# A transformer-like network with two mixtures of experts: a region of memory for each expert, routing and sending in groups of 8 tiles, expert tiles of 128 rows whose results are scattered inside the loop, plain loads in the combine

## The reference, cut to what matters

```python
def _moe(tokens, router_w, w1, b1, w2, b2):            # layer 0: hidden width 256
    logits = tokens @ router_w.T
    probs = softmax(logits); rw, re = top_k(probs, 2)
    rw = rw / maximum(rw.sum(-1), 1e-12)
    out = tokens
    for e in range(8):
        h = gelu(tokens @ w1[e] + b1[e]); y = h @ w2[e] + b2[e]
        out = out + combine[:, e:e+1] * y               # combine: rw at the two experts, else 0
# layer 1: hidden width 1024, logits = x @ Wg + bg, shares = softmax of the two best logits,
#          out = sum of share * (gelu(x @ W1[e] + b1[e]) @ W2[e] + b2[e])
x = x + attention0(ln_c(x));  t = tokens(x);  t = t + moe0(ln_t(t))
x = x + attention1(ln_c(x));  t = tokens(x);  t = t + moe1(ln_t(t));  return image(t)
```

## Time and profile before

| | us |
|---|---|
| median of 3 runs | 2737.84 |
| the profiled execution | 2757.99 |
| its span (first to last instruction) | 2756.3 |
| TensorE busy | 2073.8 (75%) |
| VectorE busy | 2053.9 (75%) |
| ScalarE busy | 1503.3 (55%) |
| GpSimd busy | 908.0 (33%) |
| mean granted TensorE clock | 0.859 of full speed |

### The profile page before, as it was taken

The page is one execution under the profiler, slowest core; times in us unless marked ns, Lnnn a source line. Parts: engine busy times, 40 slices in busy tenths (PEclk is TensorE's granted clock), DMA queues, the critical chain, the costliest instruction groups (busy, mean ns, idle before and its releaser), DMA issues. The chain is left out here.

```text
span 2756.3 us, 80547 instructions
## 1 busy us (share of the span) xinstructions
PE 2073.8 (75%) x26686; PEld 1558.4 (57%) x26687; DVE 2053.9 (75%) x3051; ACT 1503.3 (55%) x1982; POOL 908.0 (33%) x1023
## 2 busy tenths in 40 slices
PE   4639999999999999999770593036983079999961
PEld 3327666666666666666550472013862069999951
DVE  4979999999999999999782365487985334454433
ACT  5339999999999999999421120022532233333311
POOL 2652111121111111111036445460124844455455
PEclk8869999999999999999855797557975589999975
DMA  1001111111111111111204353200003611111123
GB/s 73 0 23 31 30 30 30 30 29 27 29 29 29 30 30 30 30 30 33 66 1 162 118 159 113 75 1 1 0 0 133 232 60 46 47 52 46 46 77 126
DMA packets 235071, 147.07 MB, mean 53 GB/s; under 512 B 151873, under 2 KB 214417, under 8 KB 234769
## 3 DMA queue, kind: packets, MB, share of 16 engines
q1 hardware_dynamic: 201520, 92.48, 12.9%
q0 software_dynamic: 12288, 33.57, 3.7%
q10 hardware_dynamic: 21216, 20.45, 2.1%
HBM read 70.52 MB, written 51.64 MB: 44 GB/s over the span
## 5 line engine op out<-in xcount | busy, mean ns | idle before, releaser
L579 DVE TENSOR_TENSOR plow<-prob 128x1024 f16<-128x1024 f32 (+1 forms) x1024 | 1128.0, 1174 | 4.9 <-ACT prob L493 4.9
L493 ACT ACTIVATE prob<-scores 128x1024 f32<-128x1024 f32 x1024 | 999.1, 1026 | 91.0 <-PE scores L622 63.3
L642 PEld LDWEIGHTS outp<-vs,prob 128*128 128x128 bf16 x7680 | 516.2, 98 | 277.7 <-issue 215.7
L642 PE MATMUL outp<-vs,prob 128*128 (+1 forms) x7680 | 604.4, 193 | 26.8 <-DVE plow L579 15.9
L622 PE MATMUL scores<-qT,kT 128*128 (+1 forms) x2048 | 611.6, 380 | 7.6 <-DMA kT<-shift_rows 2.8
L644 PE MATMUL outp<-vs,plow 128*128 (+1 forms) x7680 | 601.8, 193 | 0.0
L644 PEld LDWEIGHTS outp<-vs,plow 128*128 128x128 f16 x7680 | 503.4, 97 | 59.4 <-issue 0.5
L441 POOL TENSOR_TENSOR osum<-osb 128x128 f32<-128x128 f32 x64 | 105.2, 1643 | 957.3 <-DVE rec L584 957.3
L1338 ACT ACTIVATE m1ehf<-m1eph,m1eb1c 128x256 f32<-128x256 f32 x312 | 144.8, 475 | 269.5 <-PE m1eph L1294 269.2
L1400 POOL TENSOR_TENSOR m1ehl<-m1ehf,m1ehh 128x256 f16<-128x256 f32 x312 | 211.6, 709 | 219.3 <-DVE m1ehh L1369 219.3
L1294 PE MATMUL m1eph<-m1exT,m1w 128*128 128x256 f16 x1872 | 212.3, 274 | 0.2 <-DVE m1exT L1363 0.2
(11 more groups left out here) (343 smaller groups left out, 3290.3 us busy)
## 6 DMA issues: line engine op xcount, KB each, us to landing
m1estg<-in_L_ffn_W_dram SPq DMA_DIRECT2D x16, 1024.0 KB
sorted_rows<-zero SPq DMA_DIRECT2D x64, 156.0 KB
m0exr<-sorted_rows SPq DMA_DIRECT2D x39, 256.0 KB, 2.7
expert_rows<-m0eyo ACTq DMA_DIRECT2D x39, 256.0 KB, 2.3
m1exr<-sorted_rows SPq DMA_DIRECT2D x39, 256.0 KB, 3.3
expert_rows<-m1eyo ACTq DMA_DIRECT2D x39, 256.0 KB, 3.8
staged<-qk SPq DMA_DIRECT2D x73, 128.0 KB, 2.5
tok<-in_x_dram SPq DMA_DIRECT2D x4, 1024.0 KB, 10.2
```

The costliest lines, as they stand in the source:

```text
L493: act.activation(prob[g % PBUF][:, :], scores[g % 2][:, :], ACT.Exp, scale=1.0 / (QK_SCALE * QK_SCALE)).then_inc(prob_ready, 1)
L579: dve.tensor_tensor(l[:, 0:n], p[:, 0:n], high(p)[:, 0:n], ALU.subtract).then_inc(low_ready, 1)
L642: pe.matmul(to, high(prob[g % PBUF])[:, cols], v, start=(g == 0 and i == 0 and j == 0), stop=False, skip_group_check=True)
```

## The change

Both MoE are rebuilt, with the same arithmetic on the rows:

- **Regions.** `sorted_rows` is no longer one packed list: each expert has a region of 4096 rows, one such tensor for each MoE (2 x 32896 rows). A row's place is its expert's region plus its rank there, which needs only the tokens before it. A row is 1044 bytes: the two halves, the code of the expert as first choice, and 4 copies of a target number (twice the token's number, plus one place's offset of spare rows for each of 4 buffers). Zeros now fill 2 x 534 KB for each chunk in the attention, issued at the same place.
- **`dispatch`** takes the place of norm, logits, routing, sending and weight loading, in one block. Per tile ScalarE normalizes and copies, VectorE makes both halves, TensorE transposes in float16 and multiplies by the gate. After each 8 tiles (with a lead of 3 tiles) VectorE runs the routing chain for these 8, on 128 x 64, TensorE ranks them, and GpSimd scatters them; rows lie in a ring of 16. Between the groups come weight parts (16 of 256 KB in the first MoE, two after each of the first three groups; 32 of 512 KB in the second, five after each), the rest after the last group.
- **The loop** runs over 71 tiles of 128 rows, with four buffers. SP reads a tile's first row from a table into a register. VectorE has the low halves too, and ScalarE the copy of the transposed rows. VectorE computes the 128 target rows (`aim`), and GpSimd scatters the results to `expert_rows` at 2 x token + choice (L1487). `aim` waits until the scatter that used the same buffers, four tiles ago, has landed. The load of the second bias stands at the start of this block.
- **The combine** loads plainly, 8 DMAs of 1 MB by SP in three buffers.

The diff, cut to its core:

```diff
-            def zero_rows(c):
-                sp.dma_start(sorted_dram[ds(c * ZP * ZROWS, ZP * ZROWS), :].rearrange("(p a) c -> p a c", a=ZROWS),
-                             zero[0:ZP, :, :]).then_inc(zeroed, 16)
+                for rows in sorted_rows:
+                    sp.dma_start(rows[ds(c * P * ZROWS, P * ZROWS), :].rearrange("(a p) c -> p a c", p=P),
+                                 zero[:, :, :].broadcast_to([P, ZROWS, RW])).then_inc(zeroed, 16)
...
-ET = 256
+ET = P
+REGION = S
+NR = 4
+RW = D + 1 + NR
+G = 8
+RING = 2 * G
...
+def dispatch(...):
+        LEAD = 3
+        route_after = {min(g * G + G - 1 + LEAD, NT - 1): g for g in range(NGR)}
+        early = NP * 5 // (4 * 8)
+        parts_before = [0] + [min(NP, early * (g + 1)) for g in range(NGR - 1)] + [NP]
+            def prepare(t):
+                row = halves[:, t % RING, :]
+                dve.wait_ge(xn_ready, t + 1)
+                if t >= RING:
+                    dve.wait_ge(sent[t % RING], 16 * TOP * (t // RING))
+                dve.tensor_copy(row[:, 0:D], xn[t % NX][:, :]).then_inc(hi_ready, 1)
+                if add_norm:
+                    dve.tensor_tensor(tok[:, t, :], tok[:, t, :], xn[t % NX][:, :], ALU.add)
+                dve.wait_ge(hi_ready, t + 1)
+                dve.tensor_tensor(row[:, D:2 * D], xn[t % NX][:, :], row[:, 0:D], ALU.subtract).then_inc(kept, 1)
+            for t in range(NT):
+                prepare(t)
+                if t in route_after:
+                    g = route_after[t]
+                    route(g)
+                    if g == NGR - 1:
+                        tables()
+                    for i in range(parts_before[g], parts_before[g + 1]):
+                        low(i)
+        @block.gpsimd
+        def _(pool):
+            for t in range(NT):
+                pool.wait_ge(slots_ready, t // G + 1)
+                for i in range(TOP):
+                    to = bass.IndirectOffsetOnAxis(ap=slots[t // G % 2][:, i, t % G:t % G + 1], axis=0)
+                    pool.indirect_dma_start(out=sorted_dram, out_offset=to, in_=rows[:, t % RING, :], in_offset=None
+                                            ).then_inc(sent[t % RING], 16)
...
+            def aim(i, u, it):
+                e = expert_of(dve, reg, i)
+                dve.wait_ge(x_in[u % NR], (it + u // NR) * 16 + 16)
+                sent_before = it + u // NR
+                if not (isinstance(sent_before, int) and sent_before == 0):
+                    dve.wait_ge(y_out[u % NR], sent_before * 16)
+                tail = xr[u % NR][:, D:RW]
+                dve.tensor_copy(b1c[u % NR][:, :], b1t[:, ds(e, 1), :].squeeze(1))
+                dve.scalar_tensor_tensor(out=dest[u % NR][:, :], in0=tail[:, 0:1], scalar=tile_code[:, ds(i, 1)],
+                                         in1=tail[:, 1 + u % NR:2 + u % NR], op0=ALU.not_equal, op1=ALU.add).then_inc(aimed, 1)
+            def step(i, u, it, left):
+                if left > 1:
+                    aim(i + 2, u + 2, it)
+                if left > 0:
+                    halve(i + 1, u + 1)
+                rows_out(i, u)
...
+            def step(i, u, it, left):        # GpSimd
+                pool.wait_ge(aimed, i + 1 + NR)
+                pool.wait_ge(y_taken, i + 3)
+                pool.sem_inc(sending, 1)
+                to = bass.IndirectOffsetOnAxis(ap=dest[u][:, 0:1], axis=0)
+                pool.indirect_dma_start(out=y_dram, out_offset=to, in_=yo[u][:, :], in_offset=None
+                                        ).then_inc(y_out[u], 16)
...
+def combine_experts(...):                    # GC = 4, NB = 3
+        src = y_dram[0:TOP * S, :].rearrange("(t p c) d -> p t (c d)", p=P, c=TOP)
+        def fetch(eng, q):
+            if q >= NB:
+                eng.wait_ge(added, TOP * GC * (q - NB + 1))
+            eng.dma_start(got[q % NB][:, :, :], src[:, q * GC:(q + 1) * GC, :]).then_inc(arrived[q % NB], 16)
```

More of the change, by code:

```diff
@@ new lines, in dispatch @@
+        bias = sb("bias", [P, E_N])
+        b1n = sb("b1n", [E_N * NF, P])
+        xn = [sb(f"xn{u}", [P, D]) for u in range(NX)]
+        xt = [sb(f"xt{u}", [P, 2 * KB, P], F16) for u in range(2)]
+        rows = sb("rows", [P, RING, RW])
+        halves = rows[:, :, :].bitcast(F16)
+        tails = rows[:, :, D:RW]
+        val = sb("val", A)
+        tmp = sb("tmp", A)
+        hot = sb("hot", [P, TOP, G, E_N])
+        mask = sb("mask", A, F16)
+        prod = sb("prod", [P, TOP, G, E_N])
@@ new lines, in dispatch @@
+        r = sb("r", [P, G])
+        best = sb("best", [P, TOP, G])
+        code = sb("code", [P, TOP, G])
+        place = sb("place", [P, TOP, G])
+        slots = [sb(f"slots{u}", [P, TOP, G], I32) for u in range(2)]
+        seen = [sb(f"seen{u}", [P, E_N], F16) for u in range(2)]
+        more = sb("more", [P, E_N])
+        cnt = sb("cnt", [P, E_N])
+        over = sb("over", [P, E_N, S // ET])
+        stops = [sb(f"stops{u}", [P, E_N]) for u in range(2)]
+        tiles = sb("tiles", [P, E_N])
@@ L918, in _ @@
[L918 to L946, removed]
@@ L1128, in _, with turn @@
+            g = route_after[NT - 1]
+            weigh(g)
+            for i in range(parts_before[g], parts_before[g + 1]):
+                high(i)
         @block.tensor
         def _(pe):
-            m = mask[:, :, :].rearrange("p t e -> p (t e)")
-            pe.wait_ge(step, marks["mask"])
-            pe.matmul(pt[:, 0:NT * E_N], ones[:, :], m, start=True, stop=True)
-            pe.matmul(pc[:, 0:NT * E_N], below[:, :], m, start=True, stop=True).then_inc(summed, 1)
-def experts(nc, name, F, w1, shared, rows16, slots, w1_dram, b1_dram, w2_dram, b2_dram, sorted_dram, y_dram,
-            tile_expert, ident16, ident32):
+            def turn(t):
+                pe.wait_ge(kept, t + 1)
+                if t >= 2:
+                    pe.wait_ge(xt_ready, t - 1)
+                for q in range(2 * KB):
+                    last = pe.transpose(px[t % 2][:, q, :], halves[:, t % RING, q * P:(q + 1) * P], ident16[:, :])
+                last.then_inc(turned, 1)
@@ new lines, in _ @@
+            pe.matmul(pt[:, 0:E_N], ones[:, :], seen[NGR % 2][:, :], start=True, stop=True).then_inc(totalled, 1)
+        @block.gpsimd
+        def _(pool):
+            for t in range(NT):
+                pool.wait_ge(slots_ready, t // G + 1)
[3 more added lines that the diff above has]
+                                            ).then_inc(sent[t % RING], 16)
+            for s in range(RING):
+                pool.wait_ge(sent[s], 16 * TOP * (NT // RING))
@@ L1974, in build @@
         tile_no = sb("tile_no", [P, MAXT], F32)
-        consts = (below, ones, steps, first, tile_no)
+        tok2 = sb("tok2", [P, NT], F32)
+        base = sb("base", [P, E_N], F16)
+        consts = (below, ones, steps, first, tile_no, tok2, base)
         make_identities(nc, ident32, ident16)
```

823 lines of the change are left out of this document (426 added, 397 removed).

## The result

The changed kernel took 2775.24 us (median of 4 runs, 2770.11 to 2775.58), the kernel before 2736.44 beside it: ratio 1.0138, 95% interval 1.012 to 1.0155. It is 39 us slower; the forecast was 2618. The profiled execution took 2775.58 us, its span 2773.8. That is only 17.5 us over the profiled span of before, since that execution of before was 20 us above its median.

The account below looks back on a forecast made before the run. It took GpSimd to end sending (after serial routing) and combines, TensorE the loops. Terms 1 - 40 - 46 + 59 - 12 - 38 - 46 = -122 us took the profiled 2757.99 to 2636, by the median 2616, rounded to 2618; range 2555 to 2705.

Parts of the forecast that it names:

- 0.15 for waits and register work: Second MoE's loop: added to 5.55 us of array time per half tile, giving 5.7, and 424 us for the loop.
- The prediction's own sign of being wrong: Second loop: TensorE idle by "issue", matmuls of 128 columns over 0.06 apart, would show the forecast wrong.
- The ceiling of 0.1 us a matmul: Second loop: at most 0.1 us for each of 48 first-layer matmuls, from the old loop's 11.0 us per 256 rows.
- The rival with the instruction stream: Second loop: register instructions between TensorE's matmuls become the bound, 7.5 us a tile, total 2746; chance 0.09.
- First loop: First MoE's loop: held by VectorE's wait for the scatter four tiles earlier, 2.5 us a step, 197 us against 138.
- L: First loop: time from the output's end to the scatter's landing, 2.7 to 3.2 us; two steps take this plus w.
- w: First loop: VectorE's work from its scatter wait through bias copy, target row, cast and output, 1.95 us.
- The price of the Trainium skill: First loop: about 2.0 us fixed on a GpSimd DMA, giving a 2.7 us step and a loss of 73.
- the row's 1.5: First loop: at most 1.5 us from scatter end to the waiting engine's start, read from the second MoE's last scatter.
- The half clock: First loop: rival with TensorE at 1.2 GHz, 3.2 us a half tile, loop 246 us, total 2667; chance 0.16.
- Sending: Routing and sending: scatters overlap routing, 123 us against 163 in the first MoE, 141 against 187 in the second.
- 83 + 7: First MoE's sending: 64 scatters at 1.30 us on GpSimd, 83 us, plus 7 for scatters held up by VectorE.

Follow-up runs that it names:

- run 6: Changed kernel, low tokens' product reading high weights 64 channels shifted, 46 address instructions per second-loop tile instead of 32: 9.43 us a tile, stage 692.8.
- run 1: Changed kernel with first-layer matmuls of both loops reading expert 0's w1 at a fixed address: second loop 5.48 us a tile, stage 410.7; first loop 197.3.
- run 5: Changed kernel with all first-layer matmuls reading one w1 block of the tile's expert, one address instruction per tile: second loop 5.50 us a tile, stage 411.4.
- run 10: Changed kernel with high weights in all three first-layer products, 16 address instructions per second-loop tile instead of 32: 5.72 us a tile, stage 426.4.
- run 3: Changed kernel with target rows and VectorE's scatter wait moved to right before the output operation: 2830.72 us, 1.0252 of before; first loop 3.13 us a tile.
- run 7: Changed kernel with eight buffers instead of four in both loops: 2801.78 us, 1.0238 of before; first loop 2.56 us a tile, second 8.26.
- run 11: Changed kernel with four buffers but eight steps in each loop body instead of four: second loop 8.29 us a tile, stage 609.4; first loop 2.77.

## Why the prediction was wrong

**The term that failed: a half tile of the second loop, "0.15 for waits and register work".** I had scaled the array's time by the columns and let the register work ride along. That made 5.7 us a half tile; 7.68 were measured. The prediction's own sign of being wrong came true, matmuls of 128 columns over 0.06 apart.

The runs show two streams side by side of which the longer counts. Array: 0.059 us a matmul of 128 columns, 2.8 for 48. Addresses: 4.41 us for 48 matmuls with 32 address instructions, that is, as an estimate from run 6, 0.125 for each of these and little for the matmuls between. By it they meet at about 20 addresses; 16 cost 0.2 us a tile, none of it in the matmuls, and 32 cost 7.68 - 5.50 = 2.2 us a tile, 71 x 2.2 = 155 us. Of these 2.2 us 1.6 lie in the first-layer matmuls (48 x 0.033). The other 0.6 lie outside them: from a tile's transposes to its first-layer matmuls TensorE takes 0.46 to 0.83 us in the changed kernel and 0.22 to 0.23 in run 1 (2390 to 2470 us of both). They were not taken apart further. With tiles of 256 rows the array needs 5.4 us (48 x 0.113) for the same instructions, and the price was invisible.

The ceiling of 0.1 us a matmul held (0.092), but it came from that very kernel, where the stream was not the bound, and below a ceiling I had costed the stream at nothing. The rival with the instruction stream, given 0.09 and 2746 us, was the right mechanism. That its 7.5 a tile came so near to 7.68 is in part luck: it had 4.8 for the 48 matmuls, which took 4.41, and 2.7 for the rest, which took 3.3.

**First loop.** Mechanism right, size short by 21 us. The wait was where I put it, but L, from the output's end to VectorE's going on, was 4.02 us and not 2.7 to 3.2: GpSimd begins 0.79 after the output, not 0.1 to 0.3, and from the scatter's start it takes 3.23. w was 1.68, not 1.95. With no or one address instruction (runs 1 and 5) VectorE went on 2.57 after the scatter's start (1601.43 to 1604.00 in run 1), L was 3.37 and the step 2.50 to 2.54; with 4 a tile (run 10) the step was 2.82 although the matmuls were no slower.

The DMA queues of the traces show what lies in the 0.66 us between. In the changed kernel the packets of a plain load of rows move from 1601.7 to 1602.8, and those of the scatter that began at 1600.39 from 1602.3 to 1603.1, up to 2.7 us after its start. In run 1 no load's packets move beside the scatter of 1601.43, whose own move from 1602.8 to 1603.5, up to 2.1 after its start. Two scatters before the one and four before the other show the same (in run 1 the loads begin when the scatter's packets are nearly through), and a scatter of run 10 (1600.22) has a load before it too. That the loads delay the scatter is read from this, not shown: no run moved them alone.

The price of the Trainium skill that I had set aside for the row's 1.5 ("DMA: Bandwidth & Descriptors", "Anatomy of one DMA — SWDGE (gpsimd) path"), about 2.0 us fixed, gave 2.7 a step, closer than my 2.5. But where no load stands before the scatter, VectorE goes on 2.57 - 0.96 = 1.6 us after GpSimd's instruction ends, close to the row's 1.5. The page's sum came nearer by luck: the late start (0.79) and the 0.66 us were in neither. The half clock did not come: 0.95 granted.

**Sending.** Right in both, 5 and 6 us better. The first scatter began at 1409.2, 26 us after the stage's start, as worked out:

```profile
L1259 POOL DMA_INDIRECT sorted_rows<-m0drows,m0dslots x64: 956/960/2314, 1409.2 to 1492.9; - x64
```

From there the 64 starts take 83.7 us, and my sum had 83 + 7: holding up by VectorE came to 4 us and not 7, 65.40 us busy for 64 scatters against 64 x 0.96 = 61.4. On the scatter that was held up in the earlier trace rows: the page named there, the Trainium skill's "SBUF — State Buffer", "SBUF: two separate sides", does list VectorE operations with two SBUF inputs, against GpSimd operations that read SBUF; so the prediction says too much where it has no such operation on the page.

**Combines.** Right, 5 and 7 better; VectorE's adds begin 5.8 us after the first load's issue where I had 9. **Zeros.** Right: the attention is as long with 68 MB of zeros written in place of 10, DMA share 0.30 in place of 0.14. **TensorE's own time in the first loop.** The 110 us were also too low, for the same reason as in the second: 12 matmuls there took 1.13 us, not 0.67; the scatter's wait hid most of it.

## What to carry to other kernels

Halving a matmul's columns halves only the array's part: count what the sequencer has to do between matmuls, and take its price from a run in which it is the bound, since a loop bound by the array shows none. Fixing the address in one run shows it. When a wait is costed by a DMA's landing, look at which other DMAs will move at that moment. When a wait is moved, follow what else hangs on the semaphore that moves with it (run 3), and when a loop is unrolled, look at the instruction queue's traffic.

## What was not expected of the hardware

- TensorE's address computations cost next to nothing at 16 in 48 matmuls of 128 columns (0.059 us a matmul, as with none; 0.2 us a tile), but 0.092 a matmul at 32 and 0.129 at 46, from 32 to 46 0.125 us for each address.
- A loop body of eight steps (twice the instructions) costs instruction traffic: 1.10 to 1.15 MB on the instruction queue in the second loop against 0.13, TensorE idle up to 3.7 us with nothing waited for, 0.6 us a tile or 41 to 43 us in all (runs 7 and 11). The first loop's body, with less than a third of the matmuls, did not suffer (2.77 a tile).
- GpSimd begins a scatter 0.79 us after the operation it waits for ends (1599.60 to 1600.39 above). Where a row load's packets moved just before, the scatter's last ones moved 2.7 us after its start, elsewhere 2.1.
